# Reloading mixture blocks one room at a time, and second-norm transposes in two pairs of PSUM banks

## What is computed

```python
xn = layernorm(x)
x  = x + gnn(xn) + mix(xn)            # gnn: h = xn W^T + b; out = norm * sum over edges of h[col]
x  = x + ffn(layernorm(x))            # eight experts, routed with a sigmoid router
# mix: q' k' v with a relu feature map, kv = k'^T v, attn = q' kv, then attn Wo^T + bo
```

## Time and profile before

| | |
|---|---|
| median of three runs | 1118.65 us |
| profiled execution, own time | 1116.51 us |
| its span, first to last instruction | 1114.7 us |
| TensorE busy | 1070.5 us, 96% |
| VectorE, GpSimd, ScalarE busy | 533.7, 348.5, 290.5 us |
| mean granted TensorE clock | 0.985 of full speed |
| transferred | 163.17 MB, 146 GB/s |

### The profile page before, as it was taken

One profiled execution on the slowest core, in us unless ns is written; L12 is line 12 of the kernel. 1 busy time (PEld: TensorE's weight loads), 2 busy tenths in 40 slices (PEclk: granted clock), 3 DMA queues, 4 the chain that ended last, 5 costly groups with the idle time before them and its releaser, 6 DMA issues.

```text
span 1114.7 us, 15210 instructions
## 1 busy us (share of the span) xinstructions
PE 1070.5 (96%) x5527; PEld 884.6 (79%) x5527; DVE 533.7 (48%) x1152; ACT 290.5 (26%) x445; POOL 348.5 (31%) x225
## 2 busy tenths in 40 slices
PE   8999999999999999999749999997899999999998
PEld 7887778887888888888638888875588888888887
DVE  6944756676631222333136649865143211313684
ACT  5320211112222233321122223255312211202221
POOL 4000011121220133744200259953105753600151
PEclk9999999999999999999869999999899999999999
DMA  7313012222241786444683667764025756204913
GB/s 262 95 30 104 13 40 63 65 67 68 69 129 62 242 287 247 167 151 153 246 241 151 227 203 206 206 168 116 1 84 183 239 182 242 64 26 180 401 46 128
DMA packets 135933, 163.17 MB, mean 146 GB/s; under 512 B 8534, under 2 KB 102578, under 8 KB 130738
## 3 DMA queue, kind: packets, MB, share of 16 engines
q1 hardware_dynamic: 135282, 160.33, 43.4%
q10 hardware_dynamic: 576, 1.84, 0.5%
HBM read 107.70 MB, written 54.45 MB: 145 GB/s over the span
## 4 chain that ended last, share of the span: by engine, by line
PE 80%; DMA 6%; DVE 5%; POOL 3%; ACT 2%; issue 2%; SPq 1%; ACTq 0%; DVEq 0%; POOLq 0%
PE ps L1888 7%; PE ps L2223 7%; PE ps L2225 7%; PE ps L2224 6%; PE ps L1890 6%; PE ps L1889 6%; PE ps L2134 6%; PE ps L2136 6%; PE ps L2135 6%; PE ps L2054 3%; PE ps L2056 3%; PE ps L2055 3%; PE ps L2163 3%; PE ps L2157 3%; PE ps L1898 2%; DMA mt_d<-mixH 2%
## 5 line engine op out<-in xcount | busy, mean ns | idle before, releaser
L1888 PE MATMUL ps<-w_hi,xnH 128*128 128x512 f32 x464 | 185.7, 400 | 4.7 <-DVE htmp L1624 4.7
L1890 PE MATMUL ps<-w_hi,xnL 128*128 128x512 f32 x464 | 181.8, 392 | 0.0
L1889 PE MATMUL ps<-w_lo,xnH 128*128 128x512 f32 x464 | 181.7, 392 | 0.0
L896 POOL TENSOR_TENSOR acc<-acc,cw 128x320 f32<-128x320 f32 x40 | 35.8, 894 | 252.7 <-ACT cw L1100 251.5
L1888 PEld LDWEIGHTS ps<-w_hi,xnH 128*128 128x128 f32 x464 | 87.8, 189 | 24.1 <-DVE htmp L1624 5.1
L1890 PEld LDWEIGHTS ps<-w_hi,xnL 128*128 128x128 f32 x464 | 87.6, 189 | 18.8
L1889 PEld LDWEIGHTS ps<-w_lo,xnH 128*128 128x128 f32 x464 | 87.8, 189 | 17.3
L1839 DVE TENSOR_TENSOR prd<-ps,wB 128x512 f32<-128x512 f32 (+1 forms) x24 | 14.2, 592 | 147.2 <-PE ps L2225 109.1
L980 POOL TENSOR_TENSOR guL<-guR,guH 128x1024 fp32r<-128x1024 f32 x16 | 39.8, 2508 | 92.6 <-ACT guH L1265 92.6
L2054 PE MATMUL ps<-xnH,w_hi 128*128 128x512 f32 (+1 forms) x192 | 68.1, 355 | 0.0
L2223 PE MATMUL ps<-x2H,guH 128*128 128x512 f32 (+1 forms) x192 | 67.7, 352 | 0.4 <-ACT wT L1334 0.4
(11 more groups left out here) (474 smaller groups left out, 2244.9 us busy)
## 6 DMA issues: line engine op xcount, KB each, us to landing
cR<-c_d SPq DMA_DIRECT2D x20, 640.0 KB, 4.7
foldin<-in SPq DMA_DIRECT2D x32, 256.0 KB, 2.8
guR<-in SPq DMA_DIRECT2D x16, 512.0 KB, 6.5
w_raw<-in SPq DMA_DIRECT2D x14, 512.0 KB, 6.2
c_d<-cw SPq DMA_DIRECT2D x40, 160.0 KB
wdq<-in SPq DMA_DIRECT2D x6, 1024.0 KB, 7.1
qR<-qT_d SPq DMA_DIRECT2D x20, 256.0 KB, 5.3
wd_d<-wd1H SPq DMA_DIRECT2D x5, 1024.0 KB, 6.9
```

What stands on the lines that cost most here:

```text
L1888: pe.matmul(target, xnH[:, kc, cols], wH[w][:, kc, :], start=(kc == 0), stop=False)
L1889: pe.matmul(target, xnH[:, kc, cols], wL[w][:, kc, :], start=False, stop=False)
L1890: mm = pe.matmul(target, xnL[:, kc, cols], wH[w][:, kc, :], start=False, stop=(kc == KC - 1))
```

## The change

Four things. (1) Blocks: a room is reloaded for the next group as soon as its low part is stored, between the stores of the next block; the order of the blocks in a group is 1, 3, 0, 2 instead of 1, 0, 2, 3; the counts are loaded, added to and stored one by one between them, each with a semaphore of its own; ScalarE's highs are tied to h steps by a table, behind the step's h high instead of ahead of it. (2) All other loads come after the last block: panel 0, q tiles 0 to 8, panel 1, q tile 9. VectorE waits for the second half of the q tiles in the first sums instead of ahead of its loop. (3) Transposes of even tiles go to banks 0 and 1, of odd tiles to banks 2 and 3, and wait for the low part of two tiles back; TensorE waits for the low part of tile 8 ahead of the first expert, which uses banks 0 and 1. (4) In the last ten aggregations VectorE does its sum and the norm ahead of the low part of tile t-2, and ScalarE takes the high of tile t-2 around the square root, then the counts, then the normalised rows; the first gate and up weights are split one in each of two steps.

```diff
-        MIX_MADE = ((1, 3), (0, 2), (2, 4), (3, 5))
+        MIX_MADE = ((1, 3), (3, 5), (0, 2), (2, 4))
...
-            for k in range(3):
-                if k:
-                    sp.wait_ge(own_st, 64 * k)
-                own_counts(k, True)
-                load_mix_blocks(k)
-                own_counts(k, False)
-                for n in range(4 * k, 4 * k + 4):
-                    store_mix_block(n)
+            for j in (3, 1, 0, 2):
+                load_mix_block(0, j)
+            for t in range(4):
+                load_own(t)
+            for n in range(16):
+                k, (j, q) = n // 4, MIX_MADE[n % 4]
+                sp.wait_ge(wd_hi, n + 1)
+                sp.dma_start(mt_d[q - 2, 0, :, k, :], mixH[:].bitcast(F32)).then_inc(wd_st[0], 16)
+
+                if n % 4 and k < 3:
+                    sp.wait_ge(wd_st[1], 16 * n)
+                    load_mix_block(k + 1, MIX_MADE[n % 4 - 1][0])
+                if 1 <= n <= NT - 4:
+                    sp.wait_ge(own_st, 16 * n)
+                    load_own(n + 3)
+                sp.wait_ge(wd_lo, n + 1)
+                sp.dma_start(mt_d[q - 2, 1, :, k, :], mixL[j][:].bitcast(F32)).then_inc(wd_st[1], 16)
+                if n < NT:
+                    sp.wait_ge(c_own, n + 1)
+                    sp.dma_start(c_d[n, :, n * P:(n + 1) * P], own[:, n % 4, :]).then_inc(own_st, 16)
+                if n % 4 == 3 and k < 3:
+                    sp.wait_ge(wd_st[1], 16 * (n + 1))
+                    load_mix_block(k + 1, j)
             sp.wait_ge(*made(("h", 0, NT - 1)))
-            for q in range(2):
-                load_mix_panel(q)
-            load_mix_blocks(3)
-            for n in range(12, 16):
-                store_mix_block(n)
-                load_q(n - 12)
-            for t in range(4, NT):
+            load_mix_panel(0)
+            for t in range(NT - 1):
                 load_q(t)
+            load_mix_panel(1)
+            load_q(NT - 1)
...
@@ pool
-                if k < 3:
-                    pool.wait_ge(in_own, 16 * min(4 * k + 4, NT))
-                for t in range(4 * k, min(4 * k + 4, NT)):
-                    pool.tensor_tensor(own[:, t % 4, :], own[:, t % 4, :], ident[:], ALU.add).then_inc(c_own, 1)
-                pool.wait_ge(in_d[0], 64 * (k + 1))
...
+                    for j in ((3, 1), (0,), (), (2,))[n]:
+                        pool.wait_ge(in_mix[j], 16 * (k + 1))
...
+                    if n < NT:
+                        pool.wait_ge(in_own[n % 4], 16 * (n // 4 + 1))
+                        pool.tensor_tensor(own[:, n % 4, :], own[:, n % 4, :], ident[:], ALU.add).then_inc(c_own, 1)
...
@@ scalar
+            MIX_AT = {3: (0, 1), 4: (2, 3), 6: (4,), 7: (5, 6), 8: (7,), 9: (8,), 10: (9, 10), 11: (11,), 12: (12,),
+                      13: (13, 14), 14: (15,)}
...
-                    if 3 <= NT * hf + t < 19:
-                        mix_high(NT * hf + t - 3)
...
                     h_high(hf, t)
+                    for n in MIX_AT.get(NT * hf + t, ()):
+                        mix_high(n)
...
                 t = i - NT
-                if t >= 3:
-                    for h in range(2):
-                        x2_hi(t - 3, h)
+                if t >= 2:
+                    x2_hi(t - 2, 0)
+                if t >= 0:
+                    ln2_sqrt(t)
+                if t >= 2:
+                    x2_hi(t - 2, 1)
                 if i + 2 < 2 * NT:
                     count_high(i + 2)
+                if t >= NT - 3 and t < NT - 1:
+                    gu_high(0, t - NT + 3)
                 if t >= 0:
-                    ln2_sqrt(t)
                     ln2_out(t)
-                if t == NT - 2:
-                    gu_high(0)
...
@@ vector
             def first_sums(s, r):
+                if s == 0:
+                    dve.wait_ge(in_q[1], 32 * HALF)
...
-            dve.wait_ge(in_q[1], 32 * HALF)
             seven_products(0)
...
-                if t >= 3:
-                    x2_low(t - 3)
                 add_sums(i)
...
                 if t >= 0:
                     ln2(t)
-            for t in range(NT - 3, NT):
+                if t >= 2:
+                    x2_low(t - 2)
+            for t in range(NT - 2, NT):
                 x2_low(t)
...
@@ tensor
-                    if t:
-                        pe.wait_ge(x2l, 2 * (t - 1) + h + 1)
+                    if t >= 2:
+                        pe.wait_ge(x2l, 2 * (t - 2) + h + 1)
...
-                        mm = pe.transpose(bank(2 + h)[:, k * P:(k + 1) * P], xz[h][t % 2][:, k * P:(k + 1) * P], ident[:])
+                        mm = pe.transpose(bank(2 * (t % 2) + h)[:, k * P:(k + 1) * P], xz[h][t % 2][:, k * P:(k + 1) * P], ident[:])
...
             x2_transposes(NT - 1)
+            pe.wait_ge(x2l, 2 * (NT - 1))
             expert(0, 0)
```

More of the change, by code:

```diff
@@ L360, in gps_layer @@
         in_bo = sem("in_bo")
-        in_own = sem("in_own")
+        in_own = [sem(f"in_own{k}") for k in range(4)]
+        in_mix = [sem(f"in_mix{k}") for k in range(4)]
         own_st = sem("own_st")
@@ L619, in _, with load_mix_block, load_own @@
                 sp.wait_ge(q_st[c], 16 * KC)
-            def load_mix_blocks(k):
-                if k:
[L623 to L632, removed]
+            def load_mix_block(k, j):
+                sp.dma_start(mixR[j][:], mr_d[j % 2, :, k + j // 2 * 4, :]).then_inc(in_mix[j], 16)
+            def load_own(t):
+                sp.dma_start(own[:, t % 4, :], c_d[t, :, t * P:(t + 1) * P]).then_inc(in_own[t % 4], 16)
             def load_mix_panel(q):
@@ L645, in load_q @@
                       .then_inc(in_q[t // HALF], 16)
-            def own_counts(k, load):
-                for t in range(4 * k, min(4 * k + 4, NT)):
[L650 to L655, removed]
             for w in range(NWIN - 3, NWIN):
@@ L1183, in mix_high @@
             def mix_high(n):
-                act.wait_ge(wd_mix, 4 * (n // 4) + (1, 2, 4, 3)[n % 4])
+                act.wait_ge(wd_mix, 4 * (n // 4) + (1, 3, 3, 4)[n % 4])
                 if n:
@@ L1259, in ln2_out, with gu_high @@
                                    bias=lnw[:, t % 2, 19:20]).then_inc(x2n, 1)
-            def gu_high(e):
+            def gu_high(e, g):
                 p = e % 2
-                for g in range(2):
-                    act.wait_ge(in_gu[p][g], 16 * (e // 2 + 1))
-                    act.activation(guH[:, p, g], guR[:, p, g], ACT.Copy).then_inc(gu_hi, 1)
+                act.wait_ge(in_gu[p][g], 16 * (e // 2 + 1))
+                act.activation(guH[:, p, g], guR[:, p, g], ACT.Copy).then_inc(gu_hi, 1)
             count_high(0)
@@ L1270, in _ @@
                 t = i - NT
-                if t >= 3:
-                    for h in range(2):
-                        x2_hi(t - 3, h)
+                if t >= 2:
[4 more added lines that the diff above has]
+                    x2_hi(t - 2, 1)
                 if i + 2 < 2 * NT:
                     count_high(i + 2)
+                if t >= NT - 3 and t < NT - 1:
+                    gu_high(0, t - NT + 3)
                 if t >= 0:
-                    ln2_sqrt(t)
                     ln2_out(t)
-                if t == NT - 2:
-                    gu_high(0)
-            for t in (NT - 3, NT - 2):
-                for h in range(2):
-                    x2_hi(t, h)
+            for h in range(2):
+                x2_hi(NT - 2, h)
             def z_evac(k):
@@ L1299, in _ @@
             z_evac(2)
-            gu_high(1)
+            for g in range(2):
+                gu_high(1, g)
             def gate(n):
@@ L1312, in panel_high @@
                 if k == 0:
-                    act.wait_ge(in_d[0], 256 + 32)
+                    act.wait_ge(in_d[0], 32)
                 elif k == 5:
-                    act.wait_ge(in_d[0], 256 + 80)
+                    act.wait_ge(in_d[0], 80)
                 elif k == 6:
@@ L1340, in _ @@
                 if c == 2 and e + 2 < NEXP:
-                    gu_high(e + 2)
+                    for g in range(2):
+                        gu_high(e + 2, g)
                 if n in (3, 4, 7, 9, 12, 15, 16):
@@ L1747, in x2_low @@
                     high = (x2H0[:, :, cols], xnH[:, 4:8, cols])[h]
-                    dve.tensor_tensor(low, bank(2 + h).rearrange("q (k n) -> q k n", k=4), high.bitcast(F32),
+                    dve.tensor_tensor(low, by4(bank(2 * (t % 2) + h)), high.bitcast(F32),
                                       ALU.subtract).then_inc(x2l, 1)
```

6 lines of the change are left out of this document (2 added, 4 removed).

## The result

The changed kernel took **1086.08 us** (median of 4 runs, 1084.87 to 1086.57), the kernel before beside it 1118.55 (1118.14 to 1118.68): ratio 0.9709, 95% interval 0.9692 to 0.9726, faster by 32.5 us or 2.9%. The forecast was 1079, with a range of 1073 to 1088. The direction and both places were right; the gain was 6.7 us smaller than the 39.2 I had worked out.

What follows compares the result with a forecast made beforehand. TensorE, busy 96% of the span, was taken as the bound, so only its waits could pay: 20.2 + 19.0 = 39.2 us gained, giving 1077.3 for the profiled execution and 1079.4 against the median, stated as 1079; range 1073 to 1088.

Steps and rivals of the forecast that it cites:

- place two: Second norm's transposes, where TensorE waited 13.1 us in eight waits: stretch of 46.1 us instead of 65.1, gain 19.0.
- place one: TensorE's 16.8 us wait before the first seven-product matmul: start at 552.1 instead of 572.38, gain 20.2 us.
- The two moved waits that I costed at nothing: Last q tiles' wait, moved to VectorE's first sums, covered with 2 us to spare; tile 8's before first expert, free.
- one group of blocks in 18.1 us: Mixture blocks: each later group of four takes 18.1 us, so the last low store goes out at 532.
- the uncertain link: Reissue and landing of a group's fourth load in the mixture blocks: 3.5 us, with rows showing 2.9 to 11.7.
- rival D: SP's single list: reloads wait for landings and block stores behind; slower than before, TensorE 80 us late at worst; chance 0.04.
- Rival B: Mixture block chain stays slow: loads take 5.2 us, chain ends at 537 instead of 532, total 1084.5; chance 0.11.
- panel and q tiles: Loads after the last low store: 3.5 lead-in, 5.0 panel, ten q loads of 0.90 us; tiles 0 to 4 landed at 549.5.
- 2.61 us from the first token to the first product: From landing of q tiles 0 to 4 to TensorE's first product matmul: 2.61 us, as before the change.
- I take it to fall, and book nothing: TensorE's clock falls in the forecast 4.0 us gap before the first product: no gain booked, 2.4 us more if it holds.
- after 2.71 it did not: Reading of the earlier trace: TensorE's clock did not fall after a gap of 2.71 us, but did after 4.71.
- Rival C: Second norm's aggregations keep a wait, 0.5 us on each of seven tiles: gain there 15.5, total 1083; chance 0.10.

Runs made afterwards that it cites:

- without the counts: Changed kernel without the ten diagonal count tiles between the blocks (no load, identity addition or store): 1085.11 us.
- the stores swapped: Changed kernel with SP issuing each block's low store ahead of the reload of the room before it and of the count's load: 1081.47 us.
- The idle matmuls: Changed kernel with 44 useless matmuls into a free bank between the last h job and the first product: 1083.32 us.
- the early panel: Changed kernel with panel 0 issued right behind the last reload and q tiles 0 to 3 behind the last four blocks' stores: 1080.39 us.
- the kernel put together from it: Changed kernel with panel 0 right behind the last reload, q tiles in pairs and 12 idle matmuls, low stores not moved first: 1080.31 us.
- the panel spread over two blocks: Changed kernel with low stores first, panel 0's halves issued behind blocks 12 and 13, q tiles in pairs and 10 idle matmuls: 1078.56 us.
- 20 idle matmuls, panel behind the blocks: Changed kernel with low stores first, q tiles in pairs after the loop and 20 idle matmuls ahead of the first product: 1078.45 us.

## Why the prediction was right, and where 7 us went

**Right: the reading.** Both waits of the earlier trace rows were what they were taken for: the one at place two went when its cause went, the one at place one shrank with the chain behind it, and their gains add. The h jobs ended at 548.1 as forecast. The two moved waits that I costed at nothing cost nothing. VectorE waited 2.50 us for the last q tiles in the first sums,

```profile
570.45 0.69 DVE L1648 TENSOR_TENSOR hs<-qR,qR 128x512 f32<-128x512 f32 x1 [2.50 <-DMA qR<-qT_d]
```

and TensorE has no gap there; the wait before the first expert isn't in the view of waits.

**The step that failed: one group of blocks in 18.1 us.** The last low store goes out at 537.56 instead of 532, 5.6 of the 7.1 us missing at place one. Of these, 1.4 lie in the first group already, which I kept at 478.1 and which ended at 479.50, as reloads and count transfers now stand between its stores too (478.16 without the counts, 477.33 with the stores swapped); the other 4 are the three later groups, 58.06 us instead of 54. Link by link in the first group that was forecast (479.50 to 499.65, 20.15 us):

| link | forecast | measured |
|---|---|---|
| last low store lands, fourth reload goes out | 2.4 | 3.35 |
| that reload lands | 3.5 | 3.1 |
| sum and first low | 2.64 | 2.7 |
| next high and its store | 0.95 | 0.8 |
| two more highs | 6.6 | 3.41 + 4.39 |
| last low and its store | 2.0 | 2.4 |

The load, which I had called the uncertain link, was nearly right. What I had taken as known was wrong. The last group shows it by contrast: no reload goes out between its stores, its two cycles of highs took 3.23 and 3.09 us, and it took 17.47 in all. I took the stores' 2.4 us from a kernel in which no reload goes out ahead of a store, though one row there was a warning: the 4.8 of the earlier trace rows is a high store, at 552.06, with two q loads issued 1.1 us ahead of it. And I counted what SP issues between the stores but not its new wait for a landing, which stands ahead of a low store that is ready. The swap shows both and takes 3.6 us away. (The first link's 3.35 us is high for its place: in seven other kernels with the same order it took 2.97 to 3.07, and in the later groups 3.27 to 3.55.) That is the mechanism of rival D at a small price: I had priced it only at its worst, and so nothing of it stood in the forecast. Rival B named the right end of the chain (537) for the wrong reason: the reloads landed in 2.9 to 3.3 us, not in 5.2. With the stores swapped the chain is still 2 us late (533.95 against 532), in the two groups that carry reloads. The longest landing of a high store was 4.2 us in the changed kernel and 4.0 in the swapped one, where 3 is usual; what stretches those I did not settle, and how much of the rest comes from company on the queue and how much from SP's wait isn't shown either.

**A smaller term: panel and q tiles.** From the last low store to the first token it took 19.1 us instead of 17.5. The part that decides in it is the q loads. The Trainium skill ("DMA: Bandwidth & Descriptors", Specifications) calls 512 B rows and up enough for line rate; measured were 301 GB/s at 512 B, 354 at 1 KB and 416 where panels move, so here 512 B rows did not reach the rate that the core can have, and the measurement decides. Loading in pairs, with rows of double length and fewer loads, was worth 1.3 us. 2.61 us from the first token to the first product was exact.

**The clock.** "I take it to fall, and book nothing" held for a gap that became 11.1 us: matmuls 0.43 us apart for 3.2 us. The idle matmuls show that this was worth 1.6 to 2.8 us. It held for the gap that I had forecast as well: behind the early panel's gap of 4.12 us the matmuls were 0.43 us apart 0.6 us after the restart. But "after 2.71 it did not" was misread from the earlier trace rows. In the kernel before, the granted clock is 1.00 when that gap ends at 776.6 and 0.50 from 777.9 on; only the eight transposes that stood right behind the gap ran at full clock, and the next instruction came at 783.24. The forecast doesn't rest on it, as I took the clock to fall.

**Place two: 47.1 us instead of 46.1.** A tile takes 5.44 us, not 5.33. The aggregation's first half takes 2.37 us behind transposes (715.82 to 718.19), and the row I took my 4.54 from the earlier trace rows had none in front of it. Seven tiles at 0.11 make 0.8 us; the rest is in the last transposes and the router. Rival C is refuted: no wait in the seven tiles.

Sum of the misses: 5.6 + 1.6 at place one, less 0.4 for the slow matmuls of before, and 1.0 at place two make 7.8; 39.2 - 7.8 is 31.4, against 31.6 between the spans.

## What to carry to other kernels

When an in-order queue gets a wait it didn't have, ask what stands ready behind it, not only whether it could block everything: here a wait for a landing ahead of a ready store held it for 1 to 2 us several times over, and issuing the store first took 3.6 us off the chain. Take a transfer's duration from rows with the same neighbours as in the new order; 2.4 us alone became 3.3 right behind a load of 256 KB. And once a gap is cut, look again at what ends last: the early panel helped until the h jobs became later than the loads, and then idle matmuls that had helped elsewhere stood in the way.

## What the runs showed of the hardware that was not expected

- A store of 256 KB with a load of 256 KB issued 0.36 to 0.43 us ahead of it on the same queue took 3.27 to 3.55 us until what waited for it went out (the last low store of a group, 19 cases in nine kernels). With the load 0.84 us ahead it was 2.97 to 3.07 in seven kernels and 3.35 in the changed one. With the store issued ahead of the load it took 2.38 to 3.17 (nine cases in three kernels).
- A store that stands behind large loads on the same queue lands late. The longest high store took 8.6 us with the early panel and 9.9 in the kernel put together from it (2 MB ahead of it), 7.5 with the panel spread over two blocks (1 MB ahead of it, 1 MB issued 1.7 us behind it), and 4.2 in the changed kernel.
- TensorE's granted clock can fall after a gap rather than in it. After a gap of 2.10 us (20 idle matmuls, panel behind the blocks) it was 1.00 until 556.3, 1.3 us after the restart, and 0.50 from 557.0 to 559.5; after 2.17 us (spread panel) it was 1.00 until 553.6, 0.8 us after the restart, and 0.50 until 557; in the kernel before, after 2.71 us, it was 1.00 at the restart at 776.6 and 0.50 from 777.9. After the gap of 1.50 us with the early panel it stayed at 1.00 until the h jobs ended at 549.9. So full speed right behind a gap doesn't show that the gap left the clock up.
